# The attention bias of batches 8 to 15 and of layers 2 to 4 as one VectorE pass per term, summed by accumulating DMAs

## The reference

```
hbias = jax.nn.relu(dist[..., None] @ Wth + bth)     # 32 hidden values for each entry of dist
qs_bias = (hbias @ Wto + bto)[..., 0]
logits = jnp.einsum('btnh,bfnh->bnft', k, q)
logits = logits + bias + qs_bias[:, None]
```

## Time and profile before

| | |
|---|---|
| runs, us | 1392.58, 1392.81, 1394.61 (median 1392.81) |
| span of the profiled execution | 1391.1 us |
| busy | PE 90%, DVE 88%, ACT 76%, POOL 60% |
| granted clock of PE, mean | 0.968 |
| DMA moved | 41.04 MB, mean 30 GB/s |

### The profile page before, as it was taken

How to read it: one execution, slowest core, us unless ns; L and a number is a source line. 1 busy time by engine, 2 the same in 40 slices (tenths; PEclk the granted TensorE clock), 3 DMA queues, 4 the chain that set the end, 5 groups by cost and what they waited for, 6 DMA issues and landing times.

```text
span 1391.1 us, 39815 instructions
## 1 busy us (share of the span) xinstructions
PE 1246.5 (90%) x11184; PEld 1035.3 (74%) x11184; DVE 1221.8 (88%) x4922; ACT 1062.8 (76%) x3353; POOL 833.3 (60%) x889
## 2 busy tenths in 40 slices
PE   1599989898989899998989898989898999799998
PEld 1377878787878787787778787878777877677776
DVE  4899989898989899998989898989898988579886
ACT  4588868787878788787878787868687866478886
POOL 3677767676767677776767676767676753111110
PEclk9799999999999999999999999999999999999999
DMA  5201000102110100021100000111101000000000
GB/s 152 67 7 31 15 27 12 29 12 76 44 31 12 31 12 22 20 67 39 35 16 16 25 13 29 57 48 27 31 12 42 12 12 9 5 23 19 23 14 9
DMA packets 69115, 41.04 MB, mean 30 GB/s; under 512 B 14840, under 2 KB 63872, under 8 KB 68992
## 3 DMA queue, kind: packets, MB, share of 16 engines
q1 hardware_dynamic: 68992, 39.84, 9.9%
HBM read 23.29 MB, written 1.05 MB: 17 GB/s over the span
## 4 chain that ended last, share of the span: by engine, by line
PE 23%; issue 23%; DVE 23%; ACT 18%; POOL 2%; DVEq 1%; DMA 1%; ACTq 0%; SPq 0%; POOLq 0%
ACT prob L802 10%; DVE bias_acc L951 4%; PE L L688 4%; ACT relu_z L785 4%; PE O L552 3%; PE M L582 3%; DVE score L998 3%; DVE qT L1123 3%; DVE hid L1073 3%; PE M L762 2%; DVE st L1016 2%; PE M L628 2%; PE T L695 2%; PE M L560 2%; ACT probT L809 1%
## 5 line engine op out<-in xcount | busy, mean ns | idle before, releaser
L802 ACT ACTIVATE prob<-score,nmax 128x128 f32<-128x128 f32 x1024 | 396.6, 390 | 182.4 <-DVE nmax L998 182.2
L1396 POOL TENSOR_TENSOR prob<-prob,rinv 128x512 f32<-128x512 f32 x256 | 293.5, 1146 | 232.1 <-DVE rinv L1006 229.7
L951 DVE SCALAR_TENSOR_TENSOR bias_acc<-relu_z,cst,bias_acc 128x512 f32<-128x512 f32 x370 | 339.1, 917 | 9.7 <-ACT relu_z L785 0.2
L785 ACT ACTIVATE relu_z<-dist_g,cst 128x512 f32<-128x512 f32 x386 | 295.0, 804 | 17.2 <-DMA cst<-cst_all 16.9
L998 DVE CUSTOM_DVE_ANT_0 score<-L,bias 128x128 f32<-128x128 f32 x1024 | 233.6, 281 | 4.0 <-PE L L528 1.5
L802 ACT ACTIVATION_READ_ACCUMULATOR prob<-score,nmax 128x1 f32 x1024 | 193.3, 189 | 0.0
L1391 POOL TENSOR_TENSOR sd<-mv,half 128x1 f32<-128x1 f32 x128 | 105.5, 824 | 120.3 <-DVE mv L1018 117.6
L538 PE MATMUL T<-ident,prob 128*128 128x128 f32 x1024 | 164.4, 285 | 4.9 <-POOL prob L1396 4.0
L552 PEld LDWEIGHTS O<-probT,v 128*64 128x64 f32 x2048 | 109.3, 136 | 60.0 <-issue 52.4
L582 PE MATMUL M<-wv,ctxT 128*128 128x512 f32 x256 | 144.1, 645 | 7.8 <-DVE hid L1073 5.1
L528 PE MATMUL L<-kT,qT 64*128 64x128 f32 x2048 | 148.7, 285 | 0.0
(11 more groups left out here) (134 smaller groups left out, 2282.8 us busy)
## 6 DMA issues: line engine op xcount, KB each, us to landing
dist_g<-in_fside_BxSxS SPq DMA_DIRECT2D x16, 256.0 KB, 2.8
mask_g<-in_mask_Bx1x1xS_ff SPq DMA_DIRECT2D x16, 256.0 KB, 3.3
ctxT<-ctxT_all SPq DMA_DIRECT2D x64, 64.0 KB, 1.9
xs<-x_all SPq DMA_DIRECT2D x64, 64.0 KB, 1.8
x_all<-xs SPq DMA_DIRECT2D x64, 64.0 KB, 1.8
wk<-in_L_xattn_Wk SPq DMA_DIRECT2D x4, 512.0 KB, 3.6
wv<-in_L_xattn_Wv SPq DMA_DIRECT2D x4, 512.0 KB, 4.7
wq<-in_L_xattn_Wq SPq DMA_DIRECT2D x4, 512.0 KB, 5.1
```

The lines of the kernel that those rows point to most:

```text
L785: nc.scalar.activation(relu_z[:, z_slot(g, k), :], dist_g[:, :, :], ACT.Relu, bias=cst[:, C_BTH + k:C_BTH + k + 1], scale=cst[:, C_WTH + k ...
L802: last = nc.scalar.activation(prob[:, c, m, :], score[:, c, m, :], ACT.Exp, bias=nmax[:, c, m:m + 1], scale=-1.0, accum_out=rsum[:, c, m:m ...
L951: vec.scalar_tensor_tensor(out=bias_acc[:, :], in0=relu_z[:, z_slot(g, k), :], scalar=weight, in1=bias_acc[:, :], op0=ALU.mult, op1=ALU.ad ...
L1396: gp.tensor_tensor(prob[:, c, :, :], prob[:, c, :, :], rinv[:, c, :].rearrange("p (m o) -> p m o", o=1).broadcast_to([P, 4, P]), ALU.mult) ...
```

## The change

`GROUP` becomes 8; `CHUNK = 4` keeps the old width for the first eight batches, and x keeps four slots (`SLOTS`). The bias of units 0 to 7 is made as before, in two chunks of four batches. From unit 8 on it is made in **halves** of eight batches, seven of them. The 32 terms are rewritten with the kink of each relu: `max(dist, tau[k]) * c[k]`, plus one common line `A + B * dist` per layer. The new function `kinks` computes tau, c, A and B for all layers at the start, in 23 DVE instructions over 4x32 columns or fewer. `half_term` is one DVE instruction per term over 1024 columns. Its result is added by a DMA from POOL's queue, alternately to `sum_even` and `sum_odd`; each such DMA waits for the one before it on the same sum. `begin_half` and `finish_half` add the line, the mask and the two sums. ACT's relus and POOL's three instructions per term are gone from unit 4 on.

```
-GROUP = 4
+GROUP = 8
+CHUNK = 4
+SLOTS = 4
...
+HALF_PLAN = plan([[0, 1, 1, 1], [1, 1, 1, 1], [1, 2, 1, 1], [1, 1, 1, 1], [1, 2, 1, 1], [1, 1, 2, 1], [1, 2, 1, 1],
+                  [1, 0, 0, 0]])
+FIRST_HALF_PLAN = plan([[0, 0, 1, 2], [0, 0, 1, 1], [1, 1, 1, 1], [1, 1, 0, 1], [1, 1, 1, 1], [1, 2, 1, 1], [1, 2, 1, 1],
+                        [1, 2, 1, 1], [1, 0, 0, 0]])
...
+def linked(half, k, back):
+    return (half - 1) * (LINKS[k % 2] * 16) + (link(k) - back) * 16
...
-        cst = sb("cst", [P, C_ALL])
+        cst = cst_all[:, 0, :]
+        sums = [sb("sum_even", [P, GROUP, P]), sb("sum_odd", [P, GROUP, P])]
+        z_half = [x_raw[:, GROUP:, :], c_raw[:, :GROUP, :], c_raw[:, GROUP:, :], x_raw[:, :GROUP, :]]
...
-            with eng.Fori(1, groups - 1) as g:
-                for i in range(GROUP):
-                    step(g, i)
+            if groups > 2:
+                with eng.Fori(1, groups - 1) as g:
+                    for i in range(GROUP):
+                        step(g, i)
...
-                    wait_first(sp, consts, z_done, vec_count(g + 2, 0), pool_clamp, pool_count(g + 2, 0))
-                    load_dist(g + 2)
-                    load_cst(g + 2, C_PW, C_ALL, cp_in)
-                    wait_first(sp, consts, bias_done, g + 2)
-                    load_wto(g + 2)
+                    wait_first(sp, consts, half_z, (g + 1) * BIAS_K)
+                    load_half_dist(g + 2)
+                    wait_first(sp, consts, bias_done, CHUNKS + g + 1)
+                    load_half_cst(g + 2)
+                    load_half_mask(g + 2)
...
+            def half_term(half_, k):
+                if k == 0:
+                    dve.wait_ge(half_in, half_ * 48)
+                    if not (isinstance(half_, int) and half_ == 1):
+                        dve.wait_ge(bias_done, half_ + CHUNKS - 1)
+                elif link(k) > 2:
+                    dve.wait_ge(z_added[k % 2], linked(half_, k, 2))
...
+                vec.tensor_scalar(sums[1][:, :, :] if k == 0 else z_half[k % 4], dist_h[:, :, :], hst[:, H_TAU + k:H_TAU + k + 1],
+                                  hst[:, H_C + k:H_C + k + 1], ALU.max, ALU.mult).then_inc(half_z, 1)
...
+            def begin_half(half_):
+                dve.wait_ge(half_in, half_ * 48)
+                vec.scalar_tensor_tensor(out=sums[0][:, :, :], in0=dist_h[:, :, :], scalar=hst[:, H_B:H_B + 1],
+                                         in1=sums[0][:, :, :], op0=ALU.mult, op1=ALU.add).then_inc(half_init, 1)
+            def finish_half(half_):
+                dve.wait_ge(z_added[0], half_ * (LINKS[0] * 16))
+                dve.wait_ge(z_added[1], half_ * (LINKS[1] * 16))
+                dve.wait_ge(scored, after(half_, -1, 4, 3))
+                vec.scalar_tensor_tensor(out=bias[:, :, :], in0=sums[0][:, :, :], scalar=hst[:, H_A:H_A + 1],
+                                         in1=sums[1][:, :, :], op0=ALU.add, op1=ALU.add).then_inc(bias_done, 1)
...
+            def add_half(half_, k):
+                a = k % 2
+                wait_first(pool, consts, half_z, (half_ - 1) * BIAS_K + (k + 1),
+                           *((half_init, half_) if k == 2 else ()),
+                           *((z_added[a], linked(half_, k, 1)) if link(k) > 1 else ()))
+                gp.dma_start(sums[a][:, :, :], z_half[k % 4], accum_op=ALU.add).then_inc(z_added[a], 16)
...
                 if cur:
                     norm(g, i, 0)
+                    add_halves(g, i, 0)
...
                 if cur:
                     norm(g, i, 1)
+                    add_halves(g, i, 1)
```

More of the change, by code:

```diff
@@ L445, in group @@
                             load_f2(l)
-                    if isinstance(gg, int) and gg == GROUPS_PER_LAYER - 1 and not last and i == 2:
+                    if isinstance(gg, int) and gg == GROUPS_PER_LAYER - 1 and not last and i == GROUP - 2:
                         wait_first(sp, consts, k_done, after(g, GROUP - 1, 2, 1))
@@ L791, in relus @@
                         relu(0, Z_BEFORE + k)
-                elif there(g, GROUP):
-                    for k in Z_PLAN[i][q] if i < GROUP else ():
-                        relu(g + 1, k)
+                if isinstance(g, int) and g == 0 and 0 <= i < CHUNK:
+                    for k in Z_PLAN[i][q]:
+                        relu(1, k)
             def exps(g, i, c):
@@ L973, in terms @@
                         term(0, TERMS_BEFORE + k)
-                elif there(g, GROUP):
-                    for k in TERM_PLAN[i][q] if i < GROUP else ():
-                        term(g + 1, k)
-                elif i in EARLY_STEPS:
+                elif isinstance(g, int) and g == 0 and 0 <= i < CHUNK:
+                    for k in TERM_PLAN[i][q]:
+                        term(1, k)
+                elif i in EARLY_STEPS and not there(g, GROUP):
                     for part in F_FIRST_PARTS[q]:
@@ new lines, in half_terms, with finish_chunk @@
+            def half_terms(g, i, q):
+                if i < GROUP and there(g, GROUP):
+                    for k in half_plan(g, i, q):
+                        half_term(g + 1, k)
+            def finish_chunk(c):
+                dve.wait_ge(pool_sum, pool_count(c + 1, 0))
+                dve.wait_ge(term_done, vec_count(c + 1, 0) if c == 0 else START_VEC_K + VEC_K)
+                vec.tensor_tensor(bias[:, c * CHUNK:(c + 1) * CHUNK, :], bias_acc[:, :].rearrange("p (b t) -> p b t", b=CHUNK),
+                                  pool_acc[:, :, :], ALU.add).then_inc(bias_done, 1)
@@ L1043, in _ @@
             dve.wait_ge(ln_rd, 1)
-            normalise_input(range(GROUP))
+            normalise_input(range(SLOTS))
+            kinks()
             for k in range(STATS_TERMS[1], TERMS_BEFORE):
@@ L1100, in step @@
                 terms(g, i, 2)
+                half_terms(g, i, 2)
+                if i == 0 and not (isinstance(g, int) and g == 0) and there(g, GROUP):
+                    begin_half(g + 1)
                 if cur:
@@ L1134, in step @@
                 if i == -1:
-                    finish_bias(0, 0)
+                    finish_chunk(0)
+                    begin_half(1)
+                if isinstance(g, int) and g == 0 and i == CHUNK - 1:
+                    finish_chunk(1)
                 if i == GROUP - 1 and there(g, GROUP):
-                    finish_bias(g + 1, 0)
+                    finish_half(g + 1)
             def f_first(g, i, part):
@@ L1441, in step @@
                     norm(g, i - 1, 3)
-                bias_too = 0 <= i < GROUP and there(g, GROUP)
+                if i == 0 and isinstance(g, int) and g == 0:
+                    for q in range(4):
+                        add_halves(g, i - 1, q)
+                elif i > 0:
+                    add_halves(g, i - 1, 3)
+                bias_too = isinstance(g, int) and g == 0 and 0 <= i < CHUNK
                 early = i in EARLY_STEPS and not there(g, GROUP)
```

305 lines of the change are left out of this document (187 added, 118 removed).

## The result

Median of four runs 1489.0 us (1486.6 to 1494.6) against 1392.7 for the kernel before on the same chip: ratio 1.070, 95% interval 1.068 to 1.073. The forecast was 1337 us, the range 1320 to 1395. The sign is wrong too.

The account below looks back on a forecast made before the run. PE's 15.84 us per unit, stretched 0.66 by DVE with its terms, plus loop back edges were taken to bound the kernel. Terms -52 - 21 - 2.6 + 3 + 6 + 11 = -55.6 us gave 1337 us, range 1320 to 1395.

Parts of the forecast that it names:

- Steady units: Steps 4 to 55, 52 units: each falls from 16.50 to 16.1 us, 0.26 above PE's own 15.84; 21 us saved.
- POOL late: Rival: roots or small loads late behind 512 KB adds, units of 16.9 us, 42 us more, 1379 us; chance 0.17.
- Back edges: Loop jumps: 13 at 5.9 us (76.5) become five at 4.9 (24.5); 52 us saved.
- the loops don't pay: Rival: a back edge grows with its body, five at 11.8 us, 34 of the 52 gone, 1372 us; chance 0.06.
- Last group: Steps 56 to 59 no longer have bias terms: 4 x 0.66, 2.6 us saved.
- Changes of half: Seven begin_half and finish_half replace finish_bias; mask and scalar loads may once be late: 3 us lost.
- Start and steps 0 to 3: Start: kinks, wide passes and begin_half, 6 us lost (0 to 12). Steps carrying old chunk and new half: 11 lost (7 to 18).
- The chain of adds: Rival: successive adds on one sum take 9.2 us per link, units of 18.4, 120 us more, 1457 us; chance 0.12.
- PE's floor: Rival: DVE and POOL drop out, all 52 steady units take 15.84 us, 13 us less, 1324 us; chance 0.18.

Follow-up runs that it names:

- e3: The changed kernel without the accumulating DMAs and the waits for them, VectorE's wide passes kept: 1354.2 us, ratio 0.973 to the kernel before.
- e12: e11 with the double term place second in steps 2 to 6, never third, and begin_half one place later: 1341.2 us, 0.964 of the kernel before.
- e1: The changed kernel with SyncE's ctxT load moved to the head of its step, ahead of xs store and load: 1437.6 us, 1.033 of the kernel before.
- e10: e1 with four sums in place of two, and 8 xs slots loaded at the head of the step: 1386.2 us, 0.995 of the kernel before.
- e11: e10 with the middle halves written out, no loop: 1367.7 us, 0.981 of the kernel before.
- e4: The kernel before with its loop body written twice, 7 trips of 8 units for 14 of 4: 1398.3 us, 1.005 of the kernel before.
- e2: The changed kernel with each accumulating DMA cut to one batch of eight, count, issues and waits kept: 1375.1 us, 0.988 of the kernel before.

## Why the prediction was wrong, point by point

*Steady units, 21 us saved.* **The step that failed.** Its parts were right or on the safe side: passes 0.81 us (taken 1.1), issues on GpSimd 0.88 (1.0), landing 5.0 (5), DVE 14.8 busy in the plain windows. In e3, without the adds, the six units of a half other than the one with the back edge and the next last 16.2 us on average, the forecast's 16.1, and e12 shows that such a unit takes 16.15 with the adds when nothing is late. What was missing is what the adds do to others. The forecast priced only an add's own landing against the next add on the same sum. It named the small loads queueing behind 512 KB adds under the rival "POOL late", at 42 us and with 0.17. The bytes cost 114 us, through three lists at once: ctxT at the end of SyncE's step (51 us, e1), and together GpSimd's in-order wait for the link before and the xs load behind the landing of a store (51 us, e1 to e10). The rival's own mark, a landing of 6 us or more, was wrong: at 5 us the ctxT transfer has already gone from 1.9 to 3.2, with peaks of 7.8. What was needed stood in the code of SyncE: within one unit the store waits for `resid2`, the xs load for the landing of that store, and ctxT for its turn behind both. The place of a doubled term was not priced as PE sees it either: with the double place third, that unit lasts 17.5 us in e3 and 18.8 in e11, and 16.15 in e12 with it second.

*Back edges, 52 us saved.* **The other step that failed.** "A body twice as long has no reason in the rows to make one longer" rested on DVE's and the other engines' gaps, all with a body of 4. PE's own branch goes from 0.2 to 4.8 us. e4 isolates it: the same number of units, half the jumps, 6 us more. In e3 a back edge with its boundary costs 9.2 to 10.4 us, not 4.9: 5 x 4.9 = 24 more than forecast. The rival "the loops don't pay" had 11.8, and a chance of 0.06. Nor were the 5.9 us of before all jump: 2.4 of them are the boundary.

*Last group.* 2.6 forecast. The 2.4 of the table (54 to 63) match it by luck: steps 56 to 59 (`resid2` 54 to 58) fall from 67.6 to 63.4 us, 4.3 less, 1.1 of it because no unit there follows a back edge any more, and the last unit of all takes 2.0 more (21.65 for 19.67; 18.94 in e3).

*Changes of half.* 3 us lost in all. The one boundary without a jump costs 2.7 us in the change (16.35 + 18.03), 2.4 in e3, and the same in e4 with the old bias: nothing is lost here, and the term was too high by 3.

*Start and steps 0 to 3.* 6 and 11 forecast. Cut at the first score tile of units 0 and 4, which is where these steps begin and end, the start goes from 59.2 to 66.4 us in the change and 67.0 in e3, and the four steps from 68.3 to 82.5 and 78.2: 7.8 and 9.9 more in e3, both inside their bounds, and 14.2 for the steps in the change, with late transfers in them. `kinks` takes 6.1 us (29.7 to 35.8), as priced.

*The other rivals.* The chain of adds did not bind as drawn: medians of 4.8 to 5.3 us, GpSimd's waits for it 42 us in all. Only 7 of 217 adds took more than 8 us (9.0 to 11.0), all beside the loads of `wk`, `wv` and `wq` for the next layer. Its place was right (a GpSimd that stands for a link holds the root). The change has PE's floor only where no bias work is; e3 has single units with bias work in which PE is busy for all of 15.54 us, but not 52 of them.

*The pages drawn on.* The Trainium skill (SBUF — State Buffer, Who interferes with whom) would have put passes at the upper end beside GpSimd. The trace agrees that the two hold each other up, and shows that the one that begins second pays: 27 of 224 passes began after an operation of GpSimd and took 1.40 us (median). The others had no such neighbour or began first and took 0.81, and where they began first it was GpSimd's `norm` that took 1.30 us in place of 1.03. The Trainium skill (DMA: Bandwidth & Descriptors, Anatomy of one DMA) gave an estimate of 3.2 us for 512 KB. The adds took 5.0, of which 2.8 are spent on each of 16 engines.

By runs, the 152 us between forecast and result: 114 from the bytes of the adds (e2), 21 from their issue on GpSimd and what waits were left (e3; the 0.26 us a unit of the forecast, 13.5 in all, was meant to hold this), and 17 from what e3 still has over the forecast: 24 for the jumps, less what other terms came out lower.

## What to carry to other kernels

When a change adds wide DMAs, list every small transfer of the other queues with its slack (when issued, behind which landing, when needed), and ask what twice its present landing time does; then move the issue ahead or add a slot before trusting any estimate. Before lengthening or shortening a loop, read the branch row of every engine, above all PE's, and the instruction queues between two back edges: here a body that goes round without loading code was worth more than fewer jumps, and no loop at all more still. When a fix gains nothing, look for the wait that took its place, and try both together.

## What the runs showed of the hardware that was not expected

- PE's branch: 0.21 us with a body of 4 units and nothing loaded on q8, 4.9 us with a body of 8 and 14 packets of 16 KB a trip (e4), 4.0 to 5.5 in the change and 3.4 to 3.7 in e3. Where between 4 and 8 it turns was not tried.
- An accumulating DMA of 512 KB inside SBUF takes 2.8 us of all 16 DMA engines and 4.8 to 5.3 us to land (medians); beside such adds a 64 KB transfer takes 3.2 us in place of 1.9 (median), 7.8 at most in the change and 12.8 in e12.
- Full DMA engines (0.92) beside a PE at 16.06 of 16.15 us (e12).
- VectorE's wide passes over one tensor and GpSimd's operations hold each other up, and the one that begins second pays: 1.40 us for a pass in place of 0.81, 1.30 for `norm` in place of 1.03 (medians, the change).
- Written out, the kernel before has one GpSimd instruction of 128x1 at 1.10 us in place of 0.55, and units longer by 0.48 us. Not explained.
